# Placing the drive products of a selective scan on VectorE and GpSimd

## The chip, the cores and the metric

The kernel runs on one core of one Trainium2 chip. The metric is the time of one execution on the device in microseconds, and of several executions the median. It holds all of the work: loading the inputs, two stages of computation and storing the result.

## What is computed

The input is a batch of 32 images of 32 x 32 pixels with 64 channels. Two layers follow, each around a residual connection and a group norm. The first is a conv layer with routing over four experts; the change doesn't touch it. The second is a pair of Mamba blocks, one along the rows of each image and one along its columns. The core of a Mamba block, cut from the reference:

```python
dt = softplus(einsum('blr,er->ble', dt, dt_w) + dt_b)
A = -exp(A_log)
def step(h, inp):
    dt_t, B_t, C_t, u_t = inp
    dA = exp(dt_t[:, :, None] * A)
    h = dA * h + dt_t[:, :, None] * B_t[:, None, :] * u_t[:, :, None]
    y = einsum('bes,bs->be', h, C_t)
    return (h, y)
...
y = ys + xc * Dvec
y = y * silu(z)
out = einsum('ble,de->bld', y, out_w)
```

There are 128 inner channels (e) and 16 states (s). Every state has its own recurrence over the 32 places of a row or column.

## The kernel before

Stage 1 is the first layer and ends some 700 us into the span. Stage 2 is the pair of Mamba blocks and takes the rest. It works in 128 **units**. A unit is half an image, 16 rows (or columns) of 32 pixels, in one of the two directions: 128 inner channels on the partitions by 512 pixels. Units of rows and of columns alternate in pairs.

In a unit the 16 states are taken two at a time, so there are eight **pairs**, 0 to 7 (`PAIRS`). For a pair p, with s = 2p the first of its states, four steps follow each other on different engines:

- **Decay**: ScalarE computes exp(dt x A) for each state into `decays` (`decay`, L1428).
- **Product** (the drive): dt x u, held in `dtx` and as a copy in PSUM in `p_dtx`, times the B of two states. The result is in the PSUM tensor `p_drive`, which holds two pairs. Six of the eight products come from VectorE (`make_drives`, L1588). Two come from GpSimd into `pool_drive` (`make_drive`, L1554), and ScalarE copies these to `p_drive` (`move_drive`, L1436). `BY_POOL` names the two by their first state: 0 and 8, that is pairs 0 and 4.
- **Scan**: VectorE runs the recurrence of the pair in one instruction (`scan_pair`, L1601). It waits for the decays, for the product (`drive_done` or `drive_moved`) and for the read of four pairs before, since `state` has room for four pairs.
- **Read**: GpSimd multiplies the states by C (`read_states`, L1537). TensorE then sums over the states with matmuls by the identity into `p_y`, one **add** per state (`add_state`, L1306), which in fp32 is two matmul instructions in the trace.

When all 16 adds of a unit are done, VectorE multiplies `p_y` by the gate silu(z): the **gate product** (`apply_gate`, L1611). Only after it may TensorE write `p_y` for the next unit (`add_skip`, L1302).

B and C of a pair are one **chunk** of 1 MB, spread over the partitions from DRAM by SyncE (`bc_all`, L1161). A chunk of the next unit is loaded when the read of the same pair in this unit is done.

The order of the work is written by hand, engine by engine, and each engine runs its own in order. ScalarE, GpSimd and TensorE go through 16 **slots** s per unit. The offsets say what comes early or late in a slot: the decay of state s + 4 (`AHEAD`), GpSimd's product of state s + 6 (`POOL_LEAD`), ScalarE's copy of the product of state s + 2 (`MOVE_LEAD`), GpSimd's read in every odd slot. TensorE adds state s - 5 in slot s (`LAG`), so the last five adds of a unit, 11 to 15, stand in slots 0 to 4 of the next unit, and the two sums that make dt (`sum_dt`, L1280 and L1282) stand in slot 0 behind add 11. In slots 9 to 12 it projects the unit after the next one (L1239 or L1245, L1255 or L1259, L1267, L1275). ScalarE turns these results into the gate and into `soft` and `relu` for dt in slots 11 to 15 (L1377 to L1421), with two loads of activation tables. In slot 15 it copies `dtx` to PSUM for the next unit. GpSimd makes `dtx` of the next unit (L1544) in slot 5.

VectorE's order is written out in `slot` of `vector_program`. In each half of a unit it is scan, product, product, scan, (gate product of the unit before), scan, product, scan. A scan that is said to wait for a pair of GpSimd waits for ScalarE's copy of it.

Of the kernel before, what the change touches and what calls it, by code (L numbers as in the profile page):

```python
# [1015 lines left out]
def stage2(nc, ctx, memory, mid_x, norm_rows, out, c, early, s1):  # L1016
# [17 lines left out]
    CHUNK = 2  # L1034
    CHUNKS = N // CHUNK
    PAIRS = N // 2
    BY_POOL = (0, 8)
    BY_DVE = tuple(p for p in range(PAIRS) if 2 * p not in BY_POOL)
    POOL_LEAD = 6
    MOVE_LEAD = 2  # L1040
# [16 lines left out]
    two, four = range(2), range(4)  # L1057
# [58 lines left out]
    def ge(eng, s, value):  # L1116

        if value > 0:
            eng.wait_ge(s, value)
# [303 lines left out]
    def decay(act, u, b, m, s):  # L1423
        if s == 0:
            act.wait_ge(dt_ready, u + 1)

        ge(act, scan_done, PAIRS * u + s // 2 + 1 - DEEP // 2)
        nc.scalar.activation(decays[:, s % DEEP, :].rearrange("p (q t) -> p q t", t=SIDE)[:, :, 1:],  # L1428
                             dt[b][:, :, 1:], ACT.Exp, scale=wa[m][:, s:s + 1]).then_inc(decay_done, 1)

    def move_drive(act, u, s):
        n = BY_POOL.index(s)
        act.wait_ge(pool_drive_done, len(BY_POOL) * u + n + 1)

        ge(act, scan_done, PAIRS * u + s // 2 - 1)
        nc.scalar.copy(p_drive[:, s % 4:s % 4 + 2, :], pool_drive[n][:]).then_inc(drive_moved, 1)  # L1436
# [19 lines left out]
    def scalar_program(act, last_root, last_apply):  # L1456
# [27 lines left out]
        def slot(u, b, before, unit, after, later):  # L1484
            for s in range(N):
# [10 lines left out]
                elif after:  # L1496
                    decay(act, u + 1, 1 - b, after[0], s + AHEAD - N)
                if s + MOVE_LEAD in BY_POOL:
                    move_drive(act, u, s + MOVE_LEAD)
                elif s + MOVE_LEAD - N in BY_POOL and after:  # L1500
                    move_drive(act, u + 1, s + MOVE_LEAD - N)
# [27 lines left out]
    def gpsimd_program(pool):  # L1529
# [17 lines left out]
        def make_drive(u, b, s):  # L1547
            n = BY_POOL.index(s)
            pool.wait_ge(bc_loaded[s // CHUNK], 16 * u + 16)
# [30 lines left out]
    def vector_program(dve, last_norm):  # L1580
        def make_drives(u, p):

            if p == BY_DVE[0]:
                dve.wait_ge(dtx_copied, u + 1)
            dve.wait_ge(bc_loaded[p], 16 * u + 16)

            ge(dve, scan_done, PAIRS * u + p - 1)
            nc.vector.tensor_tensor(p_drive[:, 2 * (p % 2):2 * (p % 2) + 2, :], bc_all[p][:, :, 0, :],  # L1588
                                    p_dtx[:].unsqueeze(1).broadcast_to([128, 2, PIX]), ALU.mult).then_inc(drive_done, 1)

        def scan_pair(u, p):

            dve.wait_ge(decay_done, N * u + 2 * p + 2)
            if p in BY_DVE:
                dve.wait_ge(drive_done, len(BY_DVE) * u + BY_DVE.index(p) + 1)
            else:
                dve.wait_ge(drive_moved, len(BY_POOL) * u + BY_POOL.index(2 * p) + 1)

            ge(dve, read_done, PAIRS * u + p + 1 - DEEP // 2)
            at = 2 * p % DEEP  # L1600
            nc.vector.tensor_tensor_scan(state[:, at:at + 2, :].rearrange("p s n -> p (s n)"),  # L1601
                                         decays[:, at:at + 2, :].rearrange("p s n -> p (s n)"),
                                         p_drive[:, 2 * (p % 2):2 * (p % 2) + 2, :].rearrange("p s n -> p (s n)"), 0.0,
                                         ALU.mult, ALU.add).then_inc(scan_done, 1)

        def apply_gate(u, b, unit):
            dve.wait_ge(y_added, N * u + N)
            dve.wait_ge(gate_ready, u + 1)

            ge(dve, proj_done, u - 1)  # L1610
            nc.vector.tensor_tensor(gated[b][:], gate[gate_of(unit)][:], p_y[:], ALU.mult).then_inc(gated_done, 1)  # L1611

        def slot(u, b, before, unit, after, later):
            if u == 1:
                for g in two:
                    dve.wait_ge(s1["stored"][g], STORED)
                nc.vector.memset(cols_in[:, :, 0:2], 0.0).then_inc(padded, 1)
            for half in two:
                p = 4 * half
                scan_pair(u, p)  # L1620
                if u == 0 and half == 0:
                    last_norm(dve, 1)
                make_drives(u, p + 1)
                if u == 0 and half == 0:
                    last_norm(dve, 2)
                make_drives(u, p + 2)
                scan_pair(u, p + 1)
                if u == 0 and half == 0:
                    last_norm(dve, 3)
                if half == 0 and before:  # L1630
                    apply_gate(u - 1, 1 - b, before)
                scan_pair(u, p + 2)
                make_drives(u, p + 3)
                scan_pair(u, p + 3)

        each_unit(dve, slot)
        apply_gate(UNITS - 1, 1, (COLS, 1, IMAGES - 1))

# [64 lines left out]
```

## Time and profile before

| | |
|---|---|
| median of three runs | 3955.54 us |
| lowest and highest of the runs | 3948.23 and 3961.82 us |
| span of the profiled execution | 3947.8 us |
| VectorE busy | 3749.1 us, 95% |
| TensorE busy (matmuls) | 3654.2 us, 93% |
| GpSimd busy | 3277.5 us, 83% |
| ScalarE busy | 2937.3 us, 74% |
| mean granted TensorE clock | 0.993 of full |

The profile is of one execution, and its 3947.8 us stand within the three runs. In the names of the profile PE is TensorE, DVE is VectorE, ACT is ScalarE, POOL is GpSimd, SP is SyncE, and L1601 is line 1601 of the kernel. In a timeline a row is one instruction or several alike in succession (x2): its start and how long it took, in us from the span's start, and in brackets how long the engine was idle before it and for what it waited. Instructions of one engine overlap a little, so the distance between two starts says more than a duration.

### The profile page before, as it was taken

What the parts mean: (1) busy time and instruction counts of PE and PEld (TensorE: products, weight loads), DVE (VectorE), ACT (ScalarE), POOL (GpSimd) and SP (SyncE); (2) the same over time, 40 slices, a digit from 0 to 9 for tenths busy, and PEclk for the clock granted to TensorE, in tenths of its full rate; (3) what the DMA queues carried; (4) which work ended last, traced back from release to release, by engine and by line L of the source; (5) the groups of instructions that cost most, each with busy time, mean ns of one, the idle gap of its engine ahead of it and who ended that gap; (6) DMA issues with size and microseconds to landing.
All of it is one profiled execution on the core that took longest, in us unless ns stands there. A gap on an engine that the chain in (4) does not pass through costs nothing. (4 is left out here: it accounts for less than half of the span.)

```text
span 3947.8 us, 34409 instructions
## 1 busy us (share of the span) xinstructions
PE 3654.2 (93%) x8780; PEld 1519.6 (38%) x8780; DVE 3749.1 (95%) x3409; ACT 2937.3 (74%) x4422; POOL 3277.5 (83%) x1542
## 2 busy tenths in 40 slices
PE   7999999899999999999999999999999999999998
PEld 3444444333333333333333333333333333333333
DVE  7778787999999999999999999999999999999998
ACT  3454554787888878888888888878888888878785
POOL 2221222899999999999999999999999999999998
PEclk9999999999999999999999999999999999999999
DMA  4142324888888888898888888888899888988886
GB/s 113 33 130 58 109 74 149 325 344 338 347 348 348 344 345 340 345 350 353 347 342 350 347 347 342 352 347 341 343 353 349 339 346 347 350 340 344 336 348 264
DMA packets 203157, 1181.06 MB, mean 299 GB/s; under 512 B 30960, under 2 KB 31760, under 8 KB 68816
## 3 DMA queue, kind: packets, MB, share of 16 engines
q1 hardware_dynamic: 200128, 1177.64, 77.5%
q10 hardware_dynamic: 2832, 1.23, 0.1%
q8 instruction: 70, 1.15, 0.1%
q14 instruction: 127, 1.04, 0.1%
HBM read 1144.03 MB, written 34.73 MB: 299 GB/s over the span
## 5 line engine op out<-in xcount | busy, mean ns | idle before, releaser
L1537 POOL TENSOR_TENSOR read<-state,bc_all 128x1024 f32<-128x1024 f32 x1024 | 2398.9, 2360 | 117.0 <-DVE state L1601 88.0
L1601 DVE TENSOR_TENSOR_SCAN state<-decays,p_drive 128x1024 f32<-128x1024 f32 x1024 | 2297.9, 2274 | 33.0 <-ACT p_drive L1436 9.8
L1306 PE MATMUL p_y<-read,ident 128*128 128x512 f32 x4096 | 1921.9, 602 | 14.0 <-POOL read L1537 13.9
L1428 ACT ACTIVATE decays<-dt,wa 128x496 f32<-128x496 f32 x2048 | 1337.2, 703 | 121.1 <-DVE state L1601 118.5
L1306 PEld LDWEIGHTS p_y<-read,ident 128*128 128x128 f32 x4096 | 764.9, 191 | 990.6 <-issue 833.2
L1588 DVE TENSOR_TENSOR p_drive<-bc_all,p_dtx 128x1024 f32<-128x1024 f32 x768 | 906.5, 1210 | 0.0
L1554 POOL TENSOR_TENSOR pool_drive<-dtx,bc_all 128x1024 f32<-128x1024 f32 x256 | 602.4, 2353 | 12.2 <-DMA bc_all<-bc_scratch 11.9
L766 POOL TENSOR_TENSOR pad<-map_all,xc 128x512 f32<-128x512 f32 x96 | 138.9, 1476 | 519.1 <-DMA map_all<-map_scratch 498.3
L1436 ACT COPY p_drive<-pool_drive 128x1024 f32<-128x1024 f32 x256 | 260.8, 1019 | 270.8 <-DVE state L1601 270.8
L1302 PE MATMUL p_y<-xconv,d_diag 128*128 128x512 f32 x256 | 144.6, 647 | 202.0 <-DVE gated L1611 202.0
L556 PE MATMUL p_conv<-pad,wm 128*128 128x512 f32 x576 | 267.5, 600 | 1.8 <-issue 1.8
L565 PE MATMUL p_conv<-shf,wm 128*128 128x512 f32 x576 | 265.5, 597 | 0.9 <-ACT shf L681 0.9
L1544 POOL TENSOR_TENSOR dtx<-dt,xconv 128x512 f32<-128x512 f32 x128 | 163.6, 1278 | 12.0 <-ACT dt L1400 12.0
L705 ACT ACTIVATE mix<-we_sb,wsel 128x768 f32<-128x768 f32 x96 | 87.2, 933 | 115.0 <-DVE wm L843 71.3
L1282 PE MATMUL p_b<-soft,ident 128*128 128x512 f32 x256 | 143.3, 642 | 28.4 <-ACT soft L1421 28.3
L1384 ACT ACTIVATE gate<-p_b 128x512 f32<-128x512 f32 x128 | 76.4, 597 | 122.0 <-PE p_b L1259 66.2
L1377 ACT ACT_TABLE_LOAD x128 | 164.2, 1283 | 2.3
L1388 ACT ACT_TABLE_LOAD x128 | 164.2, 1283 | 2.3
L556 PEld LDWEIGHTS p_conv<-pad,wm 128*128 128x128 f32 x576 | 105.0, 189 | 135.7 <-issue 115.7
L1302 PEld LDWEIGHTS p_y<-xconv,d_diag 128*128 128x128 f32 x256 | 38.1, 188 | 307.6 <-DVE gated L1611 307.1
L565 PEld LDWEIGHTS p_conv<-shf,wm 128*128 128x128 f32 x576 | 106.6, 189 | 129.6 <-issue 122.4
L1245 PE MATMUL p_a<-cols_in,w_cols 128*128 128x256 f32 x640 | 148.7, 378 | 1.0 <-issue 0.5
(162 smaller groups left out, 3214.1 us busy)
## 6 DMA issues: line engine op xcount, KB each, us to landing
bc_all<-bc_scratch SPq DMA_DIRECT2D x1024, 1024.0 KB, 7.3
map_all<-map_scratch SPq DMA_DIRECT2D x48, 512.0 KB, 5.7
norm_rows<-xn SPq DMA_DIRECT2D x32, 280.0 KB, 5.8
norm_in<-norm_rows SPq DMA_DIRECT2D x64, 140.0 KB, 6.6
norm_in<-norm_rows SPq DMA_DIRECT2D x64, 139.8 KB, 7.6
fresh<-in_x SPq DMA_DIRECT2D x32, 256.0 KB, 6.8
x<-in_x SPq DMA_DIRECT2D x32, 256.0 KB, 3.6
mid_x<-x SPq DMA_DIRECT2D x32, 256.0 KB, 6.5
```

Of the source, the lines that this page charges most:

```text
L556: nc.tensor.matmul(bank[:], w_mixed[g][a][:, 0, dx, :], padded[g][a][:, :, dx:dx + SIDE], start=(dx == 0), stop=False)
L565: mm = nc.tensor.matmul(bank[:], w_mixed[g][a][:, 1, dx, :], shifted[g][a][:, :, dx:dx + SIDE], start=False, stop=(dx == 2))
L1302: nc.tensor.matmul(p_y[:], d_diag[unit[0]][:], xconv[b][:], start=True, stop=False).then_inc(skip_added, 1)
L1306: nc.tensor.matmul(p_y[:], ident[:], read[:, s % DEEP, :], start=False, stop=(s == N - 1)).then_inc(y_added, 1)
L1377: nc.scalar.activation(same_shape(xconv[b][:], m), in_order(p_a, m), ACT.Silu, bias=wcb[m][:]).then_inc(xconv_ready, 1)
L1388: nc.scalar.preload_act_table_set("natural_log_exp_and_others")
L1428: nc.scalar.activation(decays[:, s % DEEP, :].rearrange("p (q t) -> p q t", t=SIDE)[:, :, 1:], dt[b][:, :, 1:], ACT.Exp, scale=wa[m][:, s: ...
L1436: nc.scalar.copy(p_drive[:, s % 4:s % 4 + 2, :], pool_drive[n][:]).then_inc(drive_moved, 1)
L1537: nc.gpsimd.tensor_tensor(read[:, s % DEEP:s % DEEP + 2, :], state[:, s % DEEP:s % DEEP + 2, :], bc_all[s // CHUNK][:, :, 1, :], ALU.mult) ...
L1554: nc.gpsimd.tensor_tensor(pool_drive[n][:], dtx[b][:].unsqueeze(1).broadcast_to([128, 2, PIX]), bc_all[s // CHUNK][:, :, 0, :], ALU.mult). ...
L1588: nc.vector.tensor_tensor(p_drive[:, 2 * (p % 2):2 * (p % 2) + 2, :], bc_all[p][:, :, 0, :], p_dtx[:].unsqueeze(1).broadcast_to([128, 2, P ...
L1601: nc.vector.tensor_tensor_scan(state[:, at:at + 2, :].rearrange("p s n -> p (s n)"), decays[:, at:at + 2, :].rearrange("p s n -> p (s n)") ...
```

## The change

The second product of GpSimd is pair 7's (first state 14) and no longer pair 4's (first state 8). Pair 4's product goes to VectorE. VectorE's six products, before 1 and 2, 3, 5 and 6, 7, are now 1 and 2, 3 and 4, 5 and 6, each couple between two scans. The gate product stays between scans 1 and 2. Nothing else in the source is changed; through `POOL_LEAD` and `MOVE_LEAD` the number 14 also moves GpSimd's product from slot 2 to slot 8 and ScalarE's copy from slot 6 to slot 12.

```diff
--- before.py
+++ after.py
@@ -1034,7 +1034,7 @@
     CHUNK = 2
     CHUNKS = N // CHUNK
     PAIRS = N // 2
-    BY_POOL = (0, 8)
+    BY_POOL = (0, 14)
     BY_DVE = tuple(p for p in range(PAIRS) if 2 * p not in BY_POOL)
     POOL_LEAD = 6
     MOVE_LEAD = 2
@@ -1615,23 +1615,22 @@
                 for g in two:
                     dve.wait_ge(s1["stored"][g], STORED)
                 nc.vector.memset(cols_in[:, :, 0:2], 0.0).then_inc(padded, 1)
-            for half in two:
-                p = 4 * half
+            scan_pair(u, 0)
+            if u == 0:
+                last_norm(dve, 1)
+            for p in (1, 3, 5):
+                make_drives(u, p)
+                if u == 0 and p == 1:
+                    last_norm(dve, 2)
+                make_drives(u, p + 1)
                 scan_pair(u, p)
-                if u == 0 and half == 0:
-                    last_norm(dve, 1)
-                make_drives(u, p + 1)
-                if u == 0 and half == 0:
-                    last_norm(dve, 2)
-                make_drives(u, p + 2)
+                if p == 1:
+                    if u == 0:
+                        last_norm(dve, 3)
+                    if before:
+                        apply_gate(u - 1, 1 - b, before)
                 scan_pair(u, p + 1)
-                if u == 0 and half == 0:
-                    last_norm(dve, 3)
-                if half == 0 and before:
-                    apply_gate(u - 1, 1 - b, before)
-                scan_pair(u, p + 2)
-                make_drives(u, p + 3)
-                scan_pair(u, p + 3)
+            scan_pair(u, 7)
 
         each_unit(dve, slot)
         apply_gate(UNITS - 1, 1, (COLS, 1, IMAGES - 1))
```

On VectorE, in one unit before, from the gate product to the first product of the next unit. In the names, `bc_all3` is the chunk of pair 3; a scan that waits for `drive_moved` takes a GpSimd product:

```order
L1611 TENSOR_TENSOR gated1<-gate3,p_y 128x512 [waits proj_done,gate_ready,y_added]
L1601 SCALAR_TENSOR_TENSOR state<-decays,p_drive 128x1024 [waits read_done,drive_done,decay_done]
L1588 TENSOR_TENSOR p_drive<-bc_all3,p_dtx 128x1024 [waits scan_done,bc_loaded3]
L1601 SCALAR_TENSOR_TENSOR state<-decays,p_drive 128x1024 [waits read_done,drive_done,decay_done]
L1601 SCALAR_TENSOR_TENSOR state<-decays,p_drive 128x1024 [waits read_done,drive_moved,decay_done]
L1588 TENSOR_TENSOR p_drive<-bc_all5,p_dtx 128x1024 [waits scan_done,bc_loaded5]
L1588 TENSOR_TENSOR p_drive<-bc_all6,p_dtx 128x1024 [waits scan_done,bc_loaded6]
L1601 SCALAR_TENSOR_TENSOR state<-decays,p_drive 128x1024 [waits read_done,drive_done,decay_done] x2
L1588 TENSOR_TENSOR p_drive<-bc_all7,p_dtx 128x1024 [waits scan_done,bc_loaded7]
L1601 SCALAR_TENSOR_TENSOR state<-decays,p_drive 128x1024 [waits read_done,drive_done,decay_done]
L1601 SCALAR_TENSOR_TENSOR state<-decays,p_drive 128x1024 [waits read_done,drive_moved,decay_done]
L1588 TENSOR_TENSOR p_drive<-bc_all1,p_dtx 128x1024 [waits scan_done,bc_loaded1,dtx_copied]
```

And now:

```order
L1611 TENSOR_TENSOR gated1<-gate1,p_y 128x512 [waits proj_done,gate_ready,y_added]
L1601 SCALAR_TENSOR_TENSOR state<-decays,p_drive 128x1024 [waits read_done,drive_done,decay_done]
L1588 TENSOR_TENSOR p_drive<-bc_all3,p_dtx 128x1024 [waits scan_done,bc_loaded3]
L1588 TENSOR_TENSOR p_drive<-bc_all4,p_dtx 128x1024 [waits scan_done,bc_loaded4]
L1601 SCALAR_TENSOR_TENSOR state<-decays,p_drive 128x1024 [waits read_done,drive_done,decay_done] x2
L1588 TENSOR_TENSOR p_drive<-bc_all5,p_dtx 128x1024 [waits scan_done,bc_loaded5]
L1588 TENSOR_TENSOR p_drive<-bc_all6,p_dtx 128x1024 [waits scan_done,bc_loaded6]
L1601 SCALAR_TENSOR_TENSOR state<-decays,p_drive 128x1024 [waits read_done,drive_done,decay_done] x2
L1601 SCALAR_TENSOR_TENSOR state<-decays,p_drive 128x1024 [waits read_done,drive_moved,decay_done] x2
L1588 TENSOR_TENSOR p_drive<-bc_all1,p_dtx 128x1024 [waits scan_done,bc_loaded1,dtx_copied]
```

Product 4 now stands beside product 3, product 7 is gone, and the scans of pairs 7 and 0, which both wait for a copy by ScalarE, follow each other directly.

On GpSimd, from read 0 to read 5 of one unit, before (`bc_all4` in a read is the C of pair 4, in a product the B):

```order
L1537 TENSOR_TENSOR read<-state,bc_all0 128x1024 [waits scan_done,y_added,bc_loaded0]
L1554 TENSOR_TENSOR pool_drive1<-dtx1,bc_all4 128x1024 [waits drive_moved,bc_loaded4]
L1537 TENSOR_TENSOR read<-state,bc_all1 128x1024 [waits scan_done,y_added,bc_loaded1]
L1537 TENSOR_TENSOR read<-state,bc_all2 128x1024 [waits scan_done,y_added,bc_loaded2]
L1544 TENSOR_TENSOR dtx0<-dt0,xconv0 128x512 [waits dtx_copied,dt_ready]
L1537 TENSOR_TENSOR read<-state,bc_all3 128x1024 [waits scan_done,y_added,bc_loaded3]
L1537 TENSOR_TENSOR read<-state,bc_all4 128x1024 [waits scan_done,y_added,bc_loaded4]
L1554 TENSOR_TENSOR pool_drive0<-dtx0,bc_all0 128x1024 [waits drive_moved,dtx_ready,bc_loaded0]
L1537 TENSOR_TENSOR read<-state,bc_all5 128x1024 [waits scan_done,y_added,bc_loaded5]
```

And now:

```order
L1537 TENSOR_TENSOR read<-state,bc_all0 128x1024 [waits scan_done,y_added,bc_loaded0]
L1537 TENSOR_TENSOR read<-state,bc_all1 128x1024 [waits scan_done,y_added,bc_loaded1]
L1537 TENSOR_TENSOR read<-state,bc_all2 128x1024 [waits scan_done,y_added,bc_loaded2]
L1544 TENSOR_TENSOR dtx0<-dt0,xconv0 128x512 [waits dtx_copied,dt_ready]
L1537 TENSOR_TENSOR read<-state,bc_all3 128x1024 [waits scan_done,y_added,bc_loaded3]
L1554 TENSOR_TENSOR pool_drive1<-dtx1,bc_all7 128x1024 [waits drive_moved,bc_loaded7]
L1537 TENSOR_TENSOR read<-state,bc_all4 128x1024 [waits scan_done,y_added,bc_loaded4]
L1554 TENSOR_TENSOR pool_drive0<-dtx0,bc_all0 128x1024 [waits drive_moved,dtx_ready,bc_loaded0]
L1537 TENSOR_TENSOR read<-state,bc_all5 128x1024 [waits scan_done,y_added,bc_loaded5]
```

The second product has moved from between reads 0 and 1 to between reads 3 and 4. Behind read 4 stands, as before, the first product of the next unit (`dtx0`, `bc_all0`).

On ScalarE, from the middle of a unit to the steps for dt (L1414, L1415) near its end, before:

```order
L1436 COPY p_drive<-pool_drive1 128x1024 [waits scan_done,pool_drive_done]
L1428 ACTIVATE decays<-dt1,wa0 128x16x31 [waits scan_done] x2
L1465 COPY rows_out<-p_a 64x16x32 [waits cols_ready,proj_done]
L1428 ACTIVATE decays<-dt1,wa0 128x16x31 [waits scan_done] x3
L1377 ACT_TABLE_LOAD [waits dtx_ready,skip_added]
L1377 ACTIVATE xconv1<-p_a,wcb1 128x512 [waits conv_done]
L1384 ACTIVATE gate1<-p_b 128x512 [waits gated_done,z_done]
L1388 ACT_TABLE_LOAD
L1428 ACTIVATE decays<-dt0,wa1 128x16x31 [waits scan_done,dt_ready]
L1428 ACTIVATE decays<-dt0,wa1 128x16x31 [waits scan_done]
L1394 COPY bc_rows1<-p_a 32x512 [waits bc_done,rows_stored]
L1414 ACTIVATE soft<-p_b,wdtb1 128x512 [waits dt_summed,dtraw_done]
```

And now:

```order
L1465 COPY rows_out<-p_a 64x16x32 [waits cols_ready,proj_done]
L1428 ACTIVATE decays<-dt0,wa1 128x16x31 [waits scan_done] x3
L1377 ACT_TABLE_LOAD [waits dtx_ready,skip_added]
L1377 ACTIVATE xconv0<-p_a,wcb0 128x512 [waits conv_done]
L1384 ACTIVATE gate2<-p_b 128x512 [waits gated_done,z_done]
L1388 ACT_TABLE_LOAD
L1428 ACTIVATE decays<-dt1,wa1 128x16x31 [waits scan_done,dt_ready]
L1436 COPY p_drive<-pool_drive1 128x1024 [waits scan_done,pool_drive_done]
L1428 ACTIVATE decays<-dt1,wa1 128x16x31 [waits scan_done]
L1394 COPY bc_rows0<-p_a 32x512 [waits bc_done,rows_stored]
L1414 ACTIVATE soft<-p_b,wdtb0 128x512 [waits dt_summed,dtraw_done]
L1415 ACTIVATE relu<-p_b,wdtb0 128x512
```

The copy of `pool_drive1` has moved from its place ahead of the decays of L1428 x2 to one behind the gate's two activations and the second table load, and ahead of the rows copy, abs and relu (L1394, L1414, L1415).

## Rows read from the trace of the kernel before

**Rows 1.** The page: engines' busy time, two costly groups, the chunk loads.

```profile
PE 3654.2 (93%) x8780; PEld 1519.6 (38%) x8780; DVE 3749.1 (95%) x3409; ACT 2937.3 (74%) x4422; POOL 3277.5 (83%) x1542
...
L1537 POOL TENSOR_TENSOR read<-state,bc_all 128x1024 f32<-128x1024 f32 x1024 | 2398.9, 2360 | 117.0 <-DVE state L1601 88.0
...
L1544 POOL TENSOR_TENSOR dtx<-dt,xconv 128x512 f32<-128x512 f32 x128 | 163.6, 1278 | 12.0 <-ACT dt L1400 12.0
...
bc_all<-bc_scratch SPq DMA_DIRECT2D x1024, 1024.0 KB, 7.3
```

**Rows 2.** Waits, 1000 to 3000 us: waiting < waited for: us in all, times, longest.

```profile
ACT p_drive L1436 <- DVE state L1601: 167.5, 79, 2.1
PE p_y L1302 <- DVE gated L1611: 126.8, 79, 1.9
...
DVE state L1601 <- ACT p_drive L1436: 5.3, 4, 1.3
```

**Rows 3.** The scan line, 1000 to 3000 us: durations min/median/max, first and last start.

```profile
L1601 DVE TENSOR_TENSOR_SCAN state<-decays,p_drive x634: 2257/2279/2289, 1000.6 to 2998.3; 128x1024 f32<-128x1024 f32 x159
```

**Rows 4.** VectorE's timeline in one unit: start, duration, operation, xcount [wait].

```profile
1998.08 2.28 DVE L1601 TENSOR_TENSOR_SCAN state<-decays,p_drive 128x1024 f32<-128x1024 f32 x1
2000.28 0.66 DVE L1611 TENSOR_TENSOR gated<-gate,p_y 128x512 f32<-128x512 f32 x1
2000.85 2.28 DVE L1601 TENSOR_TENSOR_SCAN state<-decays,p_drive 128x1024 f32<-128x1024 f32 x1
2003.05 1.21 DVE L1588 TENSOR_TENSOR p_drive<-bc_all,p_dtx 128x1024 f32<-128x1024 f32 x1
2004.35 4.46 DVE L1601 TENSOR_TENSOR_SCAN state<-decays,p_drive 128x1024 f32<-128x1024 f32 x2
2008.73 2.33 DVE L1588 TENSOR_TENSOR p_drive<-bc_all,p_dtx 128x1024 f32<-128x1024 f32 x2
2010.97 4.46 DVE L1601 TENSOR_TENSOR_SCAN state<-decays,p_drive 128x1024 f32<-128x1024 f32 x2
...
2016.64 4.46 DVE L1601 TENSOR_TENSOR_SCAN state<-decays,p_drive 128x1024 f32<-128x1024 f32 x2
...
2023.27 2.28 DVE L1601 TENSOR_TENSOR_SCAN state<-decays,p_drive 128x1024 f32<-128x1024 f32 x1
```

**Rows 5.** GpSimd's timeline in the same unit.

```profile
2012.64 2.36 POOL L1554 TENSOR_TENSOR pool_drive<-dtx,bc_all 128x1024 f32<-128x1024 f32 x1 [1.11 <-DMA bc_all<-bc_scratch]
2014.95 9.32 POOL L1537 TENSOR_TENSOR read<-state,bc_all 128x1024 f32<-128x1024 f32 x4
```

**Rows 6.** ScalarE's timeline in the same unit.

```profile
2011.53 0.60 ACT L1384 ACTIVATE gate<-p_b 128x512 f32<-128x512 f32 x1 [1.03 <-PE p_b L1259]
...
2017.03 1.02 ACT L1436 COPY p_drive<-pool_drive 128x1024 f32<-128x1024 f32 x1
```

**Rows 7.** TensorE's timeline in the same unit.

```profile
2001.95 2.74 PE L1306 MATMUL p_y<-read,ident 128*128 128x512 f32 x6
...
2017.37 1.98 PE L1306 MATMUL p_y<-read,ident 128*128 128x512 f32 x4 [0.42 <-POOL read L1537]
...
2020.91 3.60 PE L1306 MATMUL p_y<-read,ident 128*128 128x512 f32 x8
```

**Rows 8.** TensorE's timeline around three of its gaps.

```profile
1444.05 1.13 PE L1302 MATMUL p_y<-xconv,d_diag 128*128 128x512 f32 x2 [1.90 <-DVE gated L1611]
1445.01 4.43 PE L1306 MATMUL p_y<-read,ident 128*128 128x512 f32 x6
...
3909.75 7.28 PE L1306 MATMUL p_y<-read,ident 128*128 128x512 f32 x12 [2.64 <-POOL read L1537]
3919.72 1.78 PE L1302 MATMUL p_y<-xconv,d_diag 128*128 128x512 f32 x2 [2.69 <-DVE gated L1611]
```

**Rows 9.** Short stretches: engines' busy time, then granted TensorE clock, DMA share, GB/s.

```profile
1446.00:1448.00 2.00, 2.00 (x3) 0.67 (x2) 1.91 (x3) 1.72 (x3) 1.90 (x2) 0.50 0.49 111
...
3909.70:3914.00 4.30, 4.25 (x6) 1.87 (x7) 4.21 (x3) 4.04 (x7) 3.66 (x2) 0.60 0.99 372
```

## The prediction

> **What bounds the kernel now.** I read the page's busy shares first, then the waits of a long even stretch, then the timelines of one unit, engine by engine. The reader is to see in [rows 1] that VectorE is busy 95% of the span, TensorE 93% and GpSimd 83%, and that GpSimd is filled by 1024 reads of 2.36 us; VectorE's scans take 2.28 us [rows 3]. In the waits [rows 2], taken from 1000 to 3000 us, or 79 units, VectorE waits 5.3 us in all. ScalarE waits for scans once per unit, 2.1 us each time, in front of its copy of pair 4's product. TensorE waits once per unit for the gate product, at most 1.9 us. So VectorE sets the pace, and 634 scans from 1000.6 to 2998.3 [rows 3] make (2998.3 - 1000.6) / 633 x 8 = **25.25 us per unit**. An undisturbed unit is 2023.27 - 1998.08 = 25.19 us [rows 4].
>
> The same group gives VectorE's prices, from start to start. Scan to product 2.20 (2000.85 to 2003.05); one product alone, then the scan that needs it, 1.30 (2003.05 to 2004.35); two products, then a scan, 2.24 (2008.73 to 2010.97); two scans 4.38 (2004.35 to 2008.73); gate product 0.57 (2000.28 to 2000.85). GpSimd [rows 5] starts an operation each (9.32 - 2.36) / 3 = 2.32 us. In one unit it has eight reads, two products and dtx, 10 x 2.32 + 1.28 = 24.5 us [rows 1, 5], so it is only 0.7 us from being the bound itself.
>
> **The change part by part.** *Nothing is added or removed.* Each engine has the same instructions, and the DMAs are the same. Only places change.
>
> *VectorE.* Two single products (2 x 1.30 = 2.60) become one couple (2.24). That is 0.36 us less, 25.19 - 0.36 = **24.83 us** per unit, if nothing else waits. A product alone is dearer than half a couple because its scan has to wait for its end (1.21 us long), while in a couple the second product covers that. The Trainium skill, "VectorE: DVE Perf Modes", section "The DRAIN you can't avoid", says that every VectorE instruction flushes before the next and that semaphores between them cost nothing; by that rule nothing would be saved here. The rows 1.30 against 2.24 / 2 differ from it, and the measurement decides.
>
> *ScalarE.* The copy of the last pair's product (1.02 us) [rows 6] leaves slot 6, where ScalarE had 2.1 us of waiting, and goes to slot 12, behind the gate's table load. The cover is gone. Behind it on ScalarE stand a decay, the rows copy, abs, relu, a decay, and then the copy of the next unit's first product, for which the next unit's scan 0 waits. In the trace this copy ends at 2017.03 + 1.02 = 2018.05, and scan 0 starts at 2016.64 + 2.19 = 2018.83 [rows 4, 6]: 0.78 us spare, against some 0.95 us inserted. This closes a chain: scan 0, couple, scan 1 (2.20 + 2.24 + 2.20 = 6.64), gate start to the gate's activation (2000.28 to 2011.53 = 11.25), from there to the copy's end (2018.05 - 2011.53 = 6.52), the inserted copy 0.95, hand-over 0.06, together **25.42 us**. That alone is more than 25.19, so the 0.36 us are gone already.
>
> *GpSimd and TensorE.* This is the term that counts. Before, pair 4's product stood behind read 0, where scans were not ready anyway. Now pair 7's product stands between reads 3 and 4, and the next unit's first one between reads 4 and 5. So read 5 comes four starts behind read 3, not three. TensorE's matmuls stay in order: the adds of read 5 (s = 10, 11) stand ahead of the two sums for dt and the adds 12 to 15, and VectorE's gate product waits for add 15. Behind the gate product stands scan 2, then the new couple, scan 3, and read 3 needs scan 3. The ring, from read 3 to the next read 3:
> - read 3 to the end of read 5: 4 x 2.32 + 2.36 = 11.64 [rows 5];
> - to TensorE: 2014.95 + 2.36 = 2017.31, the adds start at 2017.37 [rows 5, 7], 0.06;
> - sixteen matmul instructions (two adds, two sums, four adds, each of two): eight take 3.60 and six 2.74, so one more is 0.43, and sixteen take 3.60 + 8 x 0.43 = 7.04, plus 0.10 for the first behind a wait (four take 1.98 there, and would take 2.74 - 0.86 = 1.88 otherwise) [rows 7]; 7.14;
> - hand-over to the gate product, not seen in the trace since it never waits: 0 to 0.1, I take 0.05 as above;
> - gate 0.57, scan 2.20, couple 2.24, scan 2.28, hand-over 0.06: 7.35 [rows 4].
>
> Sum 11.64 + 0.06 + 7.14 + 0.05 + 7.35 = **26.24 us** per unit. Before, the same ring had one GpSimd start less (2.32) and one product where the couple is (0.94): 26.24 - 3.26 = 22.98 us, 2.2 under VectorE's 25.19. The trace agrees: the last adds end at 2020.91 + 3.60 = 2024.51 and the gate product comes at 2023.27 + 2.20 = 2025.47 [rows 4, 7]. The ring is the longest chain I find. The chunk loads are no part of it: they keep their order, and pair 7's product stands behind four reads and dtx after its chunk is freed, 4 x 2.32 + 1.28 = 10.6 us, while a load lands 7.3 us after its issue [rows 1]. A late one would cost its lateness; I take 0.
>
> *TensorE's clock.* Between the adds of read 4 and those of read 5 TensorE now has nothing: 2 x 2.32 less two adds (4 x 0.43 = 1.72) less the restart is a gap of some 2.8 us in every unit, right ahead of the ring's seven microseconds of matmuls. The trace shows what gaps do [rows 8, 9]. Behind the 1.90 us one at 1444.05 the granted clock is 0.50 of full (1.2 GHz in place of 2.4), and six matmuls take 4.43 us, not 2.74 [rows 7]: 1.69 us. Such gaps come in every unit, but only 4 times in 79 units did VectorE have to wait in consequence [rows 2]. Near the end there are two gaps of 2.64 and 2.69 us, the first in wait for a GpSimd read, as here, and behind both TensorE is slow: the granted clock is 0.60 over the 4.3 us behind the first, and two matmuls take 1.78 us behind the second, not 1.13. So a gap of 2.8 costs between 0 and 1.69 us of ring. One in twenty at 1.9 and two of two at 2.65 lie on both sides of what I take, nearer to the second since the gap is longer still, but two are few: **two units in three**, 0.67 x 1.69 = 1.13. The Trainium skill, "TensorE: Matmul & The Clock Gate", section "Why this matters for your kernels", warns only of idle gaps longer than these; by it the term would be 0. No gap of that length is in this trace, and the two at the end speak against it.
>
> **The sum.** 26.24 + 1.13 = 27.37 us per unit, less 25.25 is 2.12 us. Of the 128 units I leave out four at the two ends, where stage 1 still runs beside or no successor is there: 124 x 2.12 = 263 us. The profiled span is 3947.8, the median of the runs 3955.5; 3955.5 + 263 = **4218 us**.
>
> **Rivals.**
> - *The ring without the clock.* TensorE's gaps leave the clock at 2.4 GHz. 26.24 - 25.25 = 0.99, x 124 = 123: **4078 us**. For it: gaps of 1.9 us mostly do no harm. Against it: the two long gaps. The rule of the Trainium skill on idle gaps, "TensorE: Matmul & The Clock Gate", would give this case.
> - *The clock falls in every unit.* 26.24 + 1.69 - 25.25 = 2.68, x 124 = 332: **4288 us**. For it: two of two.
> - *Only ScalarE's chain binds.* That needs the ring 0.8 us shorter than summed, which one mis-sized hand-over can't give. 25.42 + 0.06 for clock falls - 25.25 = 0.23, x 124 = 29: **3984 us**.
> - *Faster: VectorE stays the bound.* The couple saves 0.36 in each unit, 124 x 0.36 = 45: **3911 us**. It needs the way from read 3 to read 5's end to be under 11.64 - (26.24 - 24.83) = 10.2 us, that is, GpSimd products of under 1.6 us where the trace has 2.36, and ScalarE's copy hidden as well. VectorE's 95% speaks for it, the two chains against it.
>
> **How the numbers follow.** Ring with the clock falling in a part of the units 0.65, in every one 0.08, ring alone 0.17, ScalarE's chain only 0.06, VectorE the bound 0.04. The likeliest gives 4218. The range takes in the ring alone and the falls in every unit, with a few us for the unknown hand-over: 4070 to 4290. A measurement of this kernel can tell about 0.3%, 12 us, from no change. Faster 0.04, same 0.02, slower 0.94.
>
> **What would show it.** In the new profile VectorE's gate product should wait for TensorE's adds about once per unit, or VectorE's busy share fall to about 88%; the adds should wait for a read some 2.8 us once per unit; reads 2 and 3 should wait for scans; TensorE's mean granted clock should fall well under 0.99; couples should still cost 2.24. If no gate product waits, the ring is wrong. If the adds wait 2.8 us and the clock stays near 0.99, only its clock term is. If scan 0 waits for the copy and nothing else does, ScalarE's chain was the bound.

## The result and the profile after

The changed kernel takes 4204.1 us (median of 4 runs, 4203.3 to 4205.7), the kernel before in the same rounds 3951.9 us. The ratio is 1.063, with a 95% interval of 1.061 to 1.065: 6.3% slower. The forecast was 4218 us, with a range of 4070 to 4290.

The page of the changed kernel, and from the list of cores its span and mean granted TensorE clock:

```profile
PE 3760.3 (89%) x8780; PEld 1560.0 (37%) x8780; DVE 3749.4 (89%) x3409; ACT 2947.2 (70%) x4422; POOL 3279.9 (78%) x1542
...
L1611 DVE TENSOR_TENSOR gated<-gate,p_y 128x512 f32<-128x512 f32 x128 | 88.0, 688 | 207.0 <-PE p_y L1306 207.0
```

```profile
core 0: 4201.5 us, clock 0.967
```

The instruction counts are those of before, and so is VectorE's busy time (3749.4 us against 3749.1): all that VectorE loses is waiting. TensorE's busy time is 106 us more (3760.3 against 3654.2), for the same matmuls at a lower clock. The gate product, which had no wait before, waits for TensorE's adds for 207 us in all, and TensorE's mean clock is 0.967 where it was 0.993.

The waits from 1000 to 3000 us answer to [rows 2] (who waits, for whom, us in all, times, longest):

```profile
POOL read L1537 <- DVE state L1601: 175.0, 109, 2.7
...
PE p_y L1306 <- POOL read L1537: 164.2, 73, 2.5
DVE gated L1611 <- PE p_y L1306: 117.9, 73, 2.4
...
DVE state L1601 <- issue: 48.8, 74, 0.9
```

There are 73 to 74 units in this stretch. TensorE waits once in each for a read, VectorE once in each for the adds, and GpSimd for scans. That is a ring in which each engine waits for the one before. (The waits of scans, put down to "issue", belong to the second chain, which the first experiment takes up.) The scan line, as in [rows 3]:

```profile
L1601 DVE TENSOR_TENSOR_SCAN state<-decays,p_drive x586: 2257/2278/2290, 998.6 to 2995.4; 128x1024 f32<-128x1024 f32 x196
```

(2995.4 - 998.6) / 585 x 8 = 27.31 us per unit, where it was 25.25; over 124 units 255 us, and 252 us were measured.

One unit in timelines, VectorE first, to be read against [rows 4]:

```profile
2007.85 2.29 DVE L1601 TENSOR_TENSOR_SCAN state<-decays,p_drive 128x1024 f32<-128x1024 f32 x1 [0.60 <-issue]
...
2016.98 0.69 DVE L1611 TENSOR_TENSOR gated<-gate,p_y 128x512 f32<-128x512 f32 x1 [2.40 <-PE p_y L1306]
2017.59 2.28 DVE L1601 TENSOR_TENSOR_SCAN state<-decays,p_drive 128x1024 f32<-128x1024 f32 x1
2019.78 2.33 DVE L1588 TENSOR_TENSOR p_drive<-bc_all,p_dtx 128x1024 f32<-128x1024 f32 x2
2022.03 4.46 DVE L1601 TENSOR_TENSOR_SCAN state<-decays,p_drive 128x1024 f32<-128x1024 f32 x2
```

GpSimd, against [rows 5]:

```profile
2024.48 2.35 POOL L1537 TENSOR_TENSOR read<-state,bc_all 128x1024 f32<-128x1024 f32 x1 [0.85 <-PE p_y L1306]
2026.78 2.36 POOL L1554 TENSOR_TENSOR pool_drive<-dtx,bc_all 128x1024 f32<-128x1024 f32 x1
2029.10 2.36 POOL L1537 TENSOR_TENSOR read<-state,bc_all 128x1024 f32<-128x1024 f32 x1
2031.41 2.36 POOL L1554 TENSOR_TENSOR pool_drive<-dtx,bc_all 128x1024 f32<-128x1024 f32 x1
2033.72 11.61 POOL L1537 TENSOR_TENSOR read<-state,bc_all 128x1024 f32<-128x1024 f32 x5
```

TensorE, against [rows 7]:

```profile
2031.76 1.88 PE L1306 MATMUL p_y<-read,ident 128*128 128x512 f32 x4
2036.13 3.59 PE L1306 MATMUL p_y<-read,ident 128*128 128x512 f32 x4 [2.50 <-POOL read L1537]
2039.56 1.02 PE L1280 MATMUL p_b<-relu,ident 128*128 128x512 f32 x2
2040.41 1.02 PE L1282 MATMUL p_b<-soft,ident 128*128 128x512 f32 x2
2041.27 3.60 PE L1306 MATMUL p_y<-read,ident 128*128 128x512 f32 x8
```

The reader can walk the ring: gate product at 2016.98, scan 2, the couple, scan 3 from 2022.03, read 3 at 2024.48, the product between reads 3 and 4, the one between reads 4 and 5, read 5 from 2033.72 to 2036.08, the adds at 2036.13, which had been waited for 2.50 us, and the last adds end at 2041.27 + 3.60 = 2044.87. The next gate product comes at 2044.91. From gate product to gate product no instruction of the ring has slack. One label misleads. The profile puts the wait of read 3 down to TensorE's adds, but by the kernel's own condition (L1533) read 3 waits for no add later than the last one of the unit before, which was done ahead of the gate product. What ends just before read 3 is scan 3, at 2022.03 + 2.28 = 2024.31.

In this unit four matmuls took 3.59 us, in a unit without a fall 1.98:

```profile
2064.07 1.98 PE L1306 MATMUL p_y<-read,ident 128*128 128x512 f32 x4 [2.05 <-POOL read L1537]
```

The granted clock behind the two gaps (behind ScalarE's and GpSimd's busy times the clock, the DMA share and GB/s), as in [rows 9]:

```profile
2064.00:2068.00 4.00, 3.94 (x9) 1.82 (x10) 4.00 (x3) 3.32 (x7) 4.00 (x3) 1.00 0.79 281
2036.00:2040.00 4.00, 3.87 (x6) 1.72 (x7) 4.00 (x3) 3.71 (x7) 4.00 (x3) 0.58 0.78 315
```

And the gate products of three units in succession:

```profile
2071.24 0.69 DVE L1611 TENSOR_TENSOR gated<-gate,p_y 128x512 f32<-128x512 f32 x1 [0.71 <-PE p_y L1306]
2099.26 0.69 DVE L1611 TENSOR_TENSOR gated<-gate,p_y 128x512 f32<-128x512 f32 x1 [2.18 <-PE p_y L1306]
2125.58 0.69 DVE L1611 TENSOR_TENSOR gated<-gate,p_y 128x512 f32<-128x512 f32 x1 [0.71 <-PE p_y L1306]
```

2099.26 - 2071.24 = 28.02 us with a fall, 2125.58 - 2099.26 = 26.32 us without. A fall costs the whole 1.70 us. The adds in front of the last two gate products:

```profile
2090.39 3.62 PE L1306 MATMUL p_y<-read,ident 128*128 128x512 f32 x4 [1.99 <-POOL read L1537]
2118.41 1.98 PE L1306 MATMUL p_y<-read,ident 128*128 128x512 f32 x4 [2.45 <-POOL read L1537]
```

Here the shorter wait brought the fall and the longer one did not. Over the 73 units whose wait is on record between 1000 and 3000 us, 18 of the 36 with a wait of about 2.0 us were long ones, and 25 of the 37 with about 2.5 us. So the length of the wait alone doesn't say whether the clock falls. What else decides is left open.

### The profile page after: what moved, and what is told of

Same layout as the page of the kernel before. It is cut to its first block, busy times and chain, and to the rows that moved or that the text cites. A ratio compares the mean times of both kernels' runs of the same rounds, so it can differ in the third digit from the quotient of the medians.

```text
span 4201.5 us, 34409 instructions
## 1 busy us (share of the span) xinstructions
PE 3760.3 (89%) x8780; PEld 1560.0 (37%) x8780; DVE 3749.4 (89%) x3409; ACT 2947.2 (70%) x4422; POOL 3279.9 (78%) x1542
## 4 chain that ended last, share of the span: by engine, by line
PE 53%; POOL 25%; DVE 16%; issue 5%; DMA 1%; POOLq 0%; ACT 0%; DVEq 0%; SPq 0%; ACTq 0%
PE p_y L1306 29%; POOL read L1537 16%; POOL pool_drive L1554 9%; DVE state L1601 7%; PE p_conv L556 4%; PE p_conv L565 4%; DVE p_drive L1588 3%; PE p_b L1280 3%; PE p_b L1282 3%; PE p_y L1302 2%; PE p_a L1245 2%; PE p_a L1315 2%; PE p_route L592 1%; DVE gated L1611 1%; PE p_b L1275 1%
## 5 line engine op out<-in xcount | busy, mean ns | idle before, releaser
L1306 PE MATMUL p_y<-read,ident 128*128 128x512 f32 x4096 | 2042.0, 628 | 290.4 <-POOL read L1537 290.4
L1428 ACT ACTIVATE decays<-dt,wa 128x496 f32<-128x496 f32 x2048 | 1347.0, 699 | 313.9 <-DVE state L1601 308.6
L1306 PEld LDWEIGHTS p_y<-read,ident 128*128 128x128 f32 x4096 | 775.4, 196 | 1329.0 <-issue 823.2
L1588 DVE TENSOR_TENSOR p_drive<-bc_all,p_dtx 128x1024 f32<-128x1024 f32 x768 | 896.3, 1212 | 0.0
L1611 DVE TENSOR_TENSOR gated<-gate,p_y 128x512 f32<-128x512 f32 x128 | 88.0, 688 | 207.0 <-PE p_y L1306 207.0
L1400 ACT COPY dt<-p_b 128x512 f32<-128x512 f32 x128 | 75.0, 586 | 186.2 <-PE p_b L1282 186.2
L1544 POOL TENSOR_TENSOR dtx<-dt,xconv 128x512 f32<-128x512 f32 x128 | 163.7, 1279 | 12.2 <-ACT dt L1400 12.2
L1474 ACT COPY result<-p_a 128x256 f32<-128x256 f32 x64 | 39.3, 614 | 161.8 <-PE p_a L1325 161.8
L1280 PE MATMUL p_b<-relu,ident 128*128 128x512 f32 x256 | 149.6, 669 | 1.4 <-ACT relu L1415 1.4
```

The costliest lines, as they stand in the source:

```text
L1280: nc.tensor.matmul(p_b[:], ident[:], relu[:], start=True, stop=False)
L1306: nc.tensor.matmul(p_y[:], ident[:], read[:, s % DEEP, :], start=False, stop=(s == N - 1)).then_inc(y_added, 1)
```

## The experiments

All are timed in three rounds beside the kernel before (3953.9 us in the first group of four, 3955.8 us in the second). "Per unit" is worked out from the scan line of each, as above. The first four start from the changed kernel.

### GpSimd's product for pair 7 ahead of read 3

```diff
-                if s + POOL_LEAD in BY_POOL:
-                    make_drive(u, b, s + POOL_LEAD)
+                if s == 6:
+                    make_drive(u, b, 14)
```

> The changed kernel, with GpSimd's product for pair 7 made ahead of read 3 (slot 6) instead of between reads 3 and 4. ScalarE's copy of it and VectorE's order stay as in the change. Ring theory: read 5 comes three GpSimd starts behind read 3 again, the ring loses 2.32 us and is 23.9 us, TensorE's gap shrinks from 2.5 to about 1.6 us and its clock goes back to over 0.985. What is left is ScalarE's chain through the two copies, 25.4 to 25.9 us per unit, so 4204 - 124 x (27.28 - 25.65) = about 4002 (3975 to 4035), with scan 0 waiting for the copy. Rival, ScalarE's late copy alone makes the change slow: the copy stands where it stood, so the time stays at 4180 to 4210.

Measured: 3994.2 us, ratio to before 1.010 (1.009 to 1.012), clock 0.996.

```profile
L1601 DVE TENSOR_TENSOR_SCAN state<-decays,p_drive x624: 2257/2279/2290, 1001.7 to 2996.9; 128x1024 f32<-128x1024 f32 x156
```

(2996.9 - 1001.7) / 623 x 8 = 25.62 us per unit. Moving one GpSimd instruction by one place gives back 210 of the 252 us. The rival, ScalarE's copy as the only cause, falls, since the copy stood where it stood. What is left is seen in front of scan 0. VectorE, then ScalarE:

```profile
2009.40 2.29 DVE L1601 TENSOR_TENSOR_SCAN state<-decays,p_drive 128x1024 f32<-128x1024 f32 x1 [0.81 <-issue]
```

```profile
2004.55 1.01 ACT L1436 COPY p_drive<-pool_drive 128x1024 f32<-128x1024 f32 x1
...
2008.31 1.00 ACT L1436 COPY p_drive<-pool_drive 128x1024 f32<-128x1024 f32 x1
```

The profile puts the wait down to "issue", but the scan starts 0.09 us behind the end of the second copy (2008.31 + 1.00 = 2009.31). The times say what the label doesn't.

What holds that chain is not always the gate's activation. One unit later, VectorE, then ScalarE:

```profile
2027.68 6.64 DVE L1601 TENSOR_TENSOR_SCAN state<-decays,p_drive 128x1024 f32<-128x1024 f32 x3
```

```profile
2030.05 1.02 ACT L1436 COPY p_drive<-pool_drive 128x1024 f32<-128x1024 f32 x1
```

The copy of pair 7's product writes the place in `p_drive` that pair 5's had, so it waits for scan 5, which starts at 2027.68 and takes 2.28 us; the copy starts 0.09 us behind its end. The gate's activation began 11.0, 11.2 or 11.5 us behind the gate product in three of every four units between 1000 and 3000 us, and in nearly all of these the copy came 14.0 us behind it and the unit took 25.51 to 25.54 us. In every fourth unit the activation came after 11.7 us; only there it was what held the copy, and the unit took 25.72 us. So the bound here is mostly VectorE's way from the gate product to scan 5, and then ScalarE's way through the two copies.

### TensorE's gap filled

```diff
+                if s == 14 and later:
+                    pe.wait_ge(rows_copied, u + 3)
+                    for _ in two:
+                        nc.tensor.matmul(p_a[:], ident[:], xconv[b][:], start=True, stop=True)
```

> The changed kernel, with two more matmuls (identity by xconv, into p_a, which nothing reads) on TensorE behind add 9 in each of 126 units, some 1.7 us of work in the gap of 2.5 us in front of add 10. No result needs them. Clock theory: the gap in front of add 10 shrinks to below 1 us, the clock falls in about one unit in twenty or less, and the ring alone is left, 26.2 to 26.35 us per unit: 4204 - 124 x (27.28 - 26.3) = about 4083 (4070 to 4100), mean granted clock over 0.985. Rival, the slow stretches lie in slack and the unit is 27.3 us for another reason: the clock goes up but the time stays at 4190 to 4215, or it grows by the added work.

Measured: 4083.2 us, ratio 1.033 (1.031 to 1.034), clock 0.995. Scan line and TensorE (L1355 is the added work):

```profile
L1605 DVE TENSOR_TENSOR_SCAN state<-decays,p_drive x608: 2257/2279/2289, 1001.7 to 2999.3; 128x1024 f32<-128x1024 f32 x152
```

```profile
2014.83 1.88 PE L1355 MATMUL p_a<-xconv,ident 128*128 128x512 f32 x4
2017.04 1.98 PE L1306 MATMUL p_y<-read,ident 128*128 128x512 f32 x4 [0.33 <-POOL read L1541]
```

26.33 us per unit. More work on the engine that is waited for makes the kernel 121 us faster, because the adds come at full clock. So of the 252 us, 121 are the clock and 131 are left with the clock up, where the gate product still waits for the adds in each of the 76 units of the stretch.

### Product 4 behind scan 3

```diff
                 make_drives(u, p)
-                make_drives(u, p + 1)
+                if p != 3:
+                    make_drives(u, p + 1)
                 scan_pair(u, p)
+                if p == 3:
+                    make_drives(u, p + 1)
```

> The changed kernel, with VectorE's product 4 behind scan 3 instead of ahead of it: the couple 3 and 4 becomes two single products, everything else as in the change. VectorE's own work grows by some 0.3 us per unit. Ring theory: the product leaves the way from the gate product to scan 3, so the ring is 0.94 us shorter (2.24 becomes 1.30) and faster although VectorE does more: 26.24 - 0.94 = 25.3 us, under ScalarE's chain of 25.4 to 26.1; with fewer falls of the clock 25.9 to 26.5 us per unit, 4035 to 4105, I take 4070. Rival, VectorE's order sets the pace and a couple saves 0.36 us: 4204 + 124 x 0.36 = 4249.

Measured: 4031.6 us, ratio 1.020 (1.018 to 1.021), clock 0.995. Waits and scan line:

```profile
DVE gated L1611 <- PE p_y L1306: 1.8, 1, 1.8
```

```profile
L1601 DVE TENSOR_TENSOR_SCAN state<-decays,p_drive x618: 2259/2279/2289, 999.7 to 2999.3; 128x1024 f32<-128x1024 f32 x155
```

25.93 us per unit. Undoing a part of the very saving that the change is about makes it 172 us faster. The gate product waits once in 77 units, so the ring isn't the bound any more. Scan 0 waits in every one:

```profile
DVE state L1601 <- issue: 46.3, 77, 0.9
```

The unit, 25.89 us when undisturbed, is 0.38 above that of the first experiment, because the single products put scan 5 later by that much and the copy of pair 7's product starts 0.1 us behind scan 5 in nearly every unit. So the 0.36 us that a couple saves show here too. The time lies just under the 4035 of the expected range: I had left a share for clock falls, and there was one in the stretch.

### Three couples with GpSimd on pairs 0 and 3

```diff
-    BY_POOL = (0, 14)
+    BY_POOL = (0, 6)
...
-                if s + POOL_LEAD in BY_POOL:
-                    make_drive(u, b, s + POOL_LEAD)
+                if s == 2:
+                    make_drive(u, b, 6)
...
             scan_pair(u, 2)
             scan_pair(u, 3)
             for p in (4, 6):
                 make_drives(u, p)
                 make_drives(u, p + 1)
                 scan_pair(u, p)
                 scan_pair(u, p + 1)
```

Scan 0, couple 1 and 2, scan 1 and the gate product stay ahead of these lines.

> Three couples on VectorE as in the change, but other pairs: GpSimd makes those of 0 and 3 and not of 0 and 7, VectorE couples 1 and 2, 4 and 5, 6 and 7. GpSimd's product for pair 3 stands in slot 2, between reads 0 and 1, where the kernel before had pair 4's. ScalarE copies it in slot 4. Ring theory: no product stands on the way from the gate product to scan 3 and only one GpSimd product between reads 3 and 5, so the ring is 26.24 - 2.32 - 2.24 = 21.7 us; ScalarE's copy is away from the table load; VectorE is the bound with three couples, 24.83 us per unit or slightly more where scan 0 waits for its copy, 24.85 to 25.0: 3952 - 124 x 0.33 = about 3911 (3900 to 3925), faster than both. Rival, a couple costs VectorE as much as two single products: 25.2 us per unit, 3945 to 3960. Rival, scans 2 and 3 in a row make GpSimd or TensorE late elsewhere: above 3960.

Measured: **3915.1 us**, ratio to before 0.990 (0.989 to 0.992), clock 0.995. It is faster than both kernels. Scan line and VectorE's timeline:

```profile
L1601 DVE TENSOR_TENSOR_SCAN state<-decays,p_drive x641: 2257/2279/2287, 1000.5 to 2999.6; 128x1024 f32<-128x1024 f32 x161
```

```profile
2007.12 2.34 DVE L1588 TENSOR_TENSOR p_drive<-bc_all,p_dtx 128x1024 f32<-128x1024 f32 x2
2009.37 2.28 DVE L1601 TENSOR_TENSOR_SCAN state<-decays,p_drive 128x1024 f32<-128x1024 f32 x1
2011.57 0.66 DVE L1611 TENSOR_TENSOR gated<-gate,p_y 128x512 f32<-128x512 f32 x1
2012.14 4.46 DVE L1601 TENSOR_TENSOR_SCAN state<-decays,p_drive 128x1024 f32<-128x1024 f32 x2
2016.52 2.33 DVE L1588 TENSOR_TENSOR p_drive<-bc_all,p_dtx 128x1024 f32<-128x1024 f32 x2
2018.76 4.46 DVE L1601 TENSOR_TENSOR_SCAN state<-decays,p_drive 128x1024 f32<-128x1024 f32 x2
```

24.99 us per unit on average. Of the 81 units in the stretch 29 take 24.80 to 24.81 us, as VectorE's sum has it; in others scan 0 comes a little later. Here no wait stands between the couples, which cost 2.24 us (2016.52 to 2018.76). So the idea of the change was sound: three couples are cheaper than two couples and two single products. It was the choice of the pairs that lost. With GpSimd on pair 7, a couple stands between the gate product and scan 3, a GpSimd product behind read 3, and ScalarE's copy behind its table load; with pair 3 none of the three does. This run removes all three at once; what the first two are worth is seen in the first and the third experiment.

### More work for ScalarE, late and early

Both start from the first experiment (3994.2 us), where the chain through ScalarE's two copies was said to be the bound. The slot is 12 in the one and 5 in the other.

```diff
+                if u > 3 and s == 12:
+                    ge(act, spare_done, u - 4)
+                    nc.scalar.copy(spare[:], w_cols[:, 0:4, :].rearrange("p k e -> p (k e)")).then_inc(spare_done, 1)
```

> The kernel with the product of pair 7 made ahead of read 3 (3994 us), with one more ScalarE instruction in 124 units: a copy of 128x512 from SBUF to SBUF that nothing reads, behind the copy of pair 7's product in slot 12. Chain theory: ScalarE's way from the gate's activation to the copy of the next unit's first product is what bounds that kernel, so the unit grows by the whole start to start time of the copy, about 0.5 us: 3994 + 124 x 0.5 = 4056 (4040 to 4070). Rival, ScalarE has slack there and something else binds: 3994 to 4005.

> The same additional copy of 128x512 on ScalarE in the same kernel, but in slot 5, where ScalarE waits for scans 1 and 2 right afterwards. Chain theory: nothing, 3990 to 4000, since only its place behind the gate's activation makes ScalarE's work count. Rival, ScalarE's sum of work is what counts: the same as with the copy in slot 12.

Measured: 4051.4 us with the copy in slot 12 (ratio 1.024, 1.023 to 1.026), 3993.2 us with the copy in slot 5 (1.009, 1.008 to 1.011). The scan lines, late and then early:

```profile
L1606 DVE TENSOR_TENSOR_SCAN state<-decays,p_drive x614: 2257/2279/2290, 1001.6 to 2998.4; 128x1024 f32<-128x1024 f32 x154
```

```profile
L1606 DVE TENSOR_TENSOR_SCAN state<-decays,p_drive x625: 2257/2279/2289, 1001.6 to 2998.3; 128x1024 f32<-128x1024 f32 x157
```

26.06 and 25.60 us per unit, against 25.62 without it. The copy in slot 12 and the two around it:

```profile
2001.67 1.02 ACT L1438 COPY p_drive<-pool_drive 128x1024 f32<-128x1024 f32 x1
2002.62 0.61 ACT L1506 COPY spare<-w_cols 128x512 f32<-128x512 f32 x1
...
2005.97 1.00 ACT L1438 COPY p_drive<-pool_drive 128x1024 f32<-128x1024 f32 x1
```

It takes 0.52 us from start to start (2002.62 to the decay at 2003.14), and the unit grows by 0.44. The same instruction seven slots earlier costs nothing. So the chain is real, and it is the bound once the ring is out of the way. As both additions stand clear of the part between the gate product and the copy of pair 7's product, they don't tell what holds that copy.

### The two sums for dt behind the adds

From the kernel with the gap filled (4083.2 us):

```diff
-              sum_dt=0, copy_dt=1, dtx=5, copy_dtx=15)
+              sum_dt=4, copy_dt=5, dtx=5, copy_dtx=15)
```

> The kernel with TensorE's gap filled (4083 us), with the two sums for dt in slot 4 of TensorE's order, behind add 15, instead of slot 0, and ScalarE's copy of dt in slot 5. Ring theory: the four matmul instructions leave the ring, 26.33 - 1.72 = 24.6 us, and ScalarE's chain of 25.6 to 25.9 us is left: 4083 - 124 x (26.33 - 25.85) = about 4023 (3995 to 4050). Rival, the ring doesn't run through TensorE's queue: no change, 4080 to 4086, or slower since dt comes later.

Measured: 4040.2 us, ratio 1.021 (1.020 to 1.023). 25.97 us per unit:

```profile
L1605 DVE TENSOR_TENSOR_SCAN state<-decays,p_drive x617: 2257/2279/2289, 999.6 to 2999.2; 128x1024 f32<-128x1024 f32 x155
```

43 us faster by a change of TensorE's order alone: the ring does run through TensorE's queue. It gives back 0.36 of the 1.72 us per unit since ScalarE's chain is next, as was expected, though 17 us above the single value that I had put down. The new order lengthens that chain itself: TensorE is still at the two sums when the gate product has ended, and the gate's activation comes 11.6 to 12.2 us behind the gate product, where it was 11.0 to 11.7.

### Half of the gap filled

```diff
-                    for _ in two:
-                        nc.tensor.matmul(p_a[:], ident[:], xconv[b][:], start=True, stop=True)
+                    nc.tensor.matmul(p_a[:], ident[:], xconv[b][:], start=True, stop=True)
```

> The kernel with the gap filled, with one additional matmul of 128x512 per unit instead of two: 0.86 us of work in the gap, which leaves a gap of about 1.6 us in front of add 10. If falls of the clock follow from long gaps, and gaps of 1.9 us gave one in twenty units and those of 2.5 us six in ten, then 1.6 us gives nearly none: 4083 to 4090, clock over 0.99. Rival, the share of falls goes with the length of the gap in proportion: about four in ten units and 4083 + 124 x 0.4 x 1.7 = 4167.

Measured: 4084.6 us, ratio 1.033 (1.031 to 1.034), clock 0.995, the same as with the whole filling. TensorE's wait that is left:

```profile
2015.75 1.98 PE L1306 MATMUL p_y<-read,ident 128*128 128x512 f32 x4 [1.19 <-POOL read L1540]
```

Gaps of 1.1 to 1.2 us in one half of the units and of 1.6 to 1.7 in the other leave the clock alone in the whole stretch from 1000 to 3000 us. The share of falls does not go with the length of the gap in proportion.

## Why the prediction was right, point by point

- *Nothing is added or removed.* Right: the counts are those of before, and so are the busy times to 10 us, but for TensorE's, which grew by 106 us with the lower clock.
- *VectorE's sum, 24.83 us.* Right, but hidden. Couples cost 2.24 to 2.25 us (2019.78 to 2022.03). The kernel with pairs 0 and 3 has 29 units of 24.80 to 24.81 us, where scan 0 comes at once, 0.38 below the 25.19 of before; its average gains 0.26. The rule of the Trainium skill, "VectorE: DVE Perf Modes", section "The DRAIN you can't avoid", by which the next instruction doesn't start until the pipe is empty and a semaphore costs nothing, is not borne out: that kernel is 39 us faster than the one before. The same section adds that a next instruction that is not held starts earlier. That would allow what the rows show, where the second product of a couple starts 1.12 us behind a first one of 1.21 us; the prediction left this exception out.
- *ScalarE's chain, 25.42 us.* Near in size, but the path was right for every fourth unit only. Its terms come out as 6.65 for scan 0 to the gate product, 11.25 to the gate's activation in a unit of the kind that was read, 7.54 from there to the copy's end (7.47 forecast) and 0.08 of hand-over (0.06), together 25.52. But in three of four units the copy of pair 7's product is held by scan 5 and not by the activation. The prediction didn't have this path, and that its length is nearly the same is luck. The average of 25.62 also has every fourth unit at 25.72 and a few longer ones.
- *The ring, 26.24 us.* Measured 26.33 in the kernels with the gap filled, 26.32 in a unit of the changed kernel without a fall. By its terms: read 3 to the end of read 5 is 2036.08 - 2024.48 = 11.60 (11.64 forecast); adds, sums, adds and hand-over are 2071.24 - 2064.07 = 7.17 (7.19); gate product to read 3 is 2024.48 - 2016.98 = 7.50 (7.35). The last is the one that was short: scan 3 ends at 2024.31, and the read starts 0.17 us behind it where I had 0.06. The check on the ring before, that "the trace agrees", was weaker than it sounds. The sum has 2.2 us of slack and the rows 2025.47 - 2024.51 = 0.96 at the gate product; another 1.11 went to GpSimd's wait for a chunk in that same unit [rows 5].
- *The gap.* 2.0 to 2.5 us in the waits, not 2.8. The adds of read 4 start at 2031.76, 0.30 us behind the read's end (2029.10 + 2.36 = 2031.46), since the projections for dt stand ahead of them, and the trace has them busy for 1.88 us where four starts take 1.72.
- *The clock.* Right in kind and near in size: a fall costs 1.70 us (1.69 forecast). The share is (27.31 - 26.33) / 1.70 = 0.58 of the units, and counted out 43 of 73, not 0.67. This share was the one large term of the sum that was chosen and not worked out, and that it came so near is partly luck. It was chosen for gaps of 2.8 us, and there were none. It also rests on a misreading: the waits of TensorE for the gate product before were of 1.9 us in 34 units and mostly of 1.4 in the others, so the four falls make one in eight or nine of the waits of 1.9, not one in twenty. The share is the largest part of the difference between 4218 and 4204: 0.09 x 1.70 x 124 = 19 us less, against 0.09 x 124 = 11 us more from the ring, and the kernel before was 4 us faster in these rounds. The rule of the Trainium skill, "TensorE: Matmul & The Clock Gate", section "Why this matters for your kernels", which warns only of longer gaps, is not borne out here: the clock fell behind waits of 2.0 to 2.5 us.
- *The rivals.* The ring without the clock was forecast at 4078 us, and the kernel with the gap filled, which is this case, took 4083. The fall in every unit (4288) didn't come. The last two were made real as well: ScalarE's chain alone (3984 forecast, 3994 measured, mostly by way of scan 5) and VectorE as the bound (3911 forecast, 3915 measured with other pairs).

## What to carry to other kernels

An engine that is busy 95% of the time is not the only one to look at: before a product is moved, close the loops through all of the engines (what must this instruction end for, and what waits for that, until you are back) and sum them. Look for every condition of an instruction, also for the place that it overwrites: that is how scan 5 held a copy here. A loop with 2.2 us of slack by the sum was closed here by moving one GpSimd instruction by a few places and putting one product ahead of a scan. When work is to be handed to another engine, choose which piece by where its neighbours on that engine are waited for. And look at what a new gap does to TensorE's clock, since the matmuls right behind the gap are the ones that someone waits for.

## What was not expected of the hardware

Added work on an engine that others wait for can pay: 0.86 us of matmuls that nothing reads, put in front of the adds in each unit, made the kernel 120 us faster, and twice as much gave the same. The clock answers to gaps steeply, but not by their length alone. Between 1000 and 3000 us, waits of up to 1.7 us gave no fall in the kernel with half of the gap filled. In the kernel before four of the 34 of 1.9 us did. In the changed kernel it was half of those of 2.0 us and two thirds of those of 2.5 us. What decides between two waits of the same length, no run here shows.
